# A gated-linear-attention layer with a split-bf16 feed-forward block: gate products moved to GpSimd, matmuls regrouped by PSUM bank, residual input added in the last group

## What is computed

```python
xn = _layernorm(x, axis=-1)
x = x + attn(xn) + relu(xn @ w1 + b1) @ w2 + b2          # w1: 1024x4096, w2: 4096x1024
# attn, 4 heads, dk = 256, dv = 512 per head:
q, k, v = xn @ Wq * dk**-0.5, xn @ Wk, xn @ Wv
gk = log_sigmoid(xn @ Wgk1 @ Wgk2 + bgk2) / 16
S = S * exp(g_t)[:, None] + k_t[:, None] * v_t[None, :];  o_t = q_t @ S    # scan over tokens
o = o * rsqrt(mean(o*o) + eps) * g_norm_weight * silu(xn @ Wg)
attn = o @ Wo
```

## Time and profile before

| | |
|---|---|
| device time, median of 2 runs | 5033.21 us (5014.32 to 5052.1) |
| profiled execution, its own time | 5015.24 us |
| its span on the slowest core (core 2) | 5013.7 us |
| spans of the 8 cores | 4989.3 to 5013.7 us |
| mean granted TensorE clock | 0.850 to 0.859 of full speed |
| TensorE / VectorE / ScalarE / GpSimd busy | 69% / 28% / 16% / 7% |

### The profile page before, as it was taken

One profiled execution on the slowest core, in us unless ns is written; L12 is line 12 of the kernel. 1 busy time (PEld: TensorE's weight loads), 2 busy tenths in 40 slices (PEclk: granted clock), 3 DMA queues, 4 the chain that ended last, 5 costly groups with the idle time before them and its releaser, 6 DMA issues.

```text
span 5013.7 us, 51334 instructions; the slowest of 8 cores (4989.3 to 5013.7 us)
## 1 busy us (share of the span) xinstructions
PE 3447.4 (69%) x17452; PEld 1990.7 (40%) x17640; DVE 1382.9 (28%) x2200; ACT 786.5 (16%) x2034; POOL 370.0 (7%) x758
## 2 busy tenths in 40 slices
PE   2000766866998666866998666866998666866998
PEld 0000435544443435544443435544443435544443
DVE  3343133133222133133222133133222133133222
ACT  4333112111000212111000212111000212111000
POOL 2232100000000000000000000000000000000000
PEclk7555778988999788988999788988999788888999
DMA  6999511211323111210323111111323111101222
GB/s 176 285 291 288 165 35 39 68 34 34 113 93 116 49 41 44 68 34 34 109 96 113 53 41 44 68 34 34 109 94 110 58 40 45 68 26 34 84 93 84
DMA packets 176738, 431.36 MB, mean 86 GB/s; under 512 B 22737, under 2 KB 55633, under 8 KB 176482
## 3 DMA queue, kind: packets, MB, share of 16 engines
q0 software_dynamic: 67584, 234.92, 14.3%
q1 hardware_dynamic: 72034, 159.57, 10.4%
q10 hardware_dynamic: 36864, 33.57, 2.5%
HBM read 352.48 MB, written 75.50 MB: 85 GB/s over the span
## 4 chain that ended last, share of the span: by engine, by line
PE 65%; DVE 13%; DMA 9%; ACT 7%; issue 6%; ACTq 0%; DVEq 0%; POOL 0%; SPq 0%; POOLq 0%
PE pb L900 13%; PE pb L549 7%; PE pb L941 5%; PE pb L944 5%; PE pb L950 4%; DVE k_sils L719 4%; PE pb L792 4%; PE pb L807 3%; PE pb L842 3%; PE pb L848 2%; PE pb L839 2%; PE pb L654 2%; PE pb L787 2%; PE pb L660 2%; PE pb L657 2%
## 5 line engine op out<-in xcount | busy, mean ns | idle before, releaser
L549 PE MATMUL pb<-t_xnfl,w_wqh 128*128 128x512 bf16 x244 | 94.5, 387 | 468.5 <-DMA w_wql<-wq_lo 467.3
L900 PE MATMUL pb<-t_xnfh,w_wvh 128*128 128x512 bf16 x1004 | 382.8, 381 | 44.3 <-DVE t_attn L967 29.4
L941 PE MATMUL pb<-w_wgh,f_h1h 128*128 128x512 bf16 x984 | 372.4, 378 | 51.0 <-DVE k_gg L909 37.9
L944 PE MATMUL pb<-w_wgl,f_h1h 128*128 128x512 bf16 x1024 | 387.7, 379 | 4.6 <-PE pb L950 2.9
L900 PE MATMUL pb<-t_xnfh,w_wvl 128*128 128x512 bf16 x1004 | 383.1, 382 | 1.3
L900 PE MATMUL pb<-t_xnfl,w_wvh 128*128 128x512 bf16 x1000 | 381.7, 382 | 1.5 <-issue 0.4
L787 PE MATMUL pb<-h_v,k_p 128*128 128x256 f32 x256 | 120.5, 620 | 319.2 <-ACT k_otm L696 183.5
L967 DVE SCALAR_TENSOR_TENSOR t_attn<-pb,t_attn 128x512 f32<-128x512 f32 x224 | 146.9, 687 | 587.0 <-PE pb L950 575.0
L654 PE MATMUL pb<-w_wvh,t_xnfh 128*128 128x256 bf16 x1024 | 288.7, 282 | 28.6 <-ACT h_spf L585 28.6
L914 ACT ACTIVATE f_h1h<-k_gg 128x512 bf16<-128x512 f32 x128 | 80.5, 629 | 1408.9 <-DVE k_gg L909 1408.9
L950 PE MATMUL pb<-w_wgh,f_h1l 128*128 128x512 bf16 x1004 | 300.2, 379 | 1.1
(11 more groups left out here) (151 smaller groups left out, 5312.1 us busy)
## 6 DMA issues: line engine op xcount, KB each, us to landing
w_wvh<-w_hi POOLq DMA_DIRECT2D x64, 512.0 KB, 3.7
w_wvl<-w_lo POOLq DMA_DIRECT2D x64, 512.0 KB, 3.6
w_wgh<-w_hi POOLq DMA_DIRECT2D x64, 512.0 KB, 4.1
w_wgl<-w_lo POOLq DMA_DIRECT2D x64, 512.0 KB, 3.6
t_x<-x SPq DMA_DIRECT2D x32, 512.0 KB, 4.7
h_v<-w_l SPq DMA_DIRECT2D x64, 256.0 KB, 12.4
h_g<-w_l SPq DMA_DIRECT2D x64, 256.0 KB, 12.5
w_wvh<-wv_hi POOLq DMA_DIRECT2D x32, 512.0 KB, 3.6
```

The costliest lines, as they stand in the source:

```text
L549: last = t.matmul(pb[bk][:, 0:PW], wgt[:, k * 128:(k + 1) * 128], mov[k][:, sl], start=first, stop=(k == 7 and wgt is wl))
L900: last = t.matmul(pb[bank][:, 0:tile_tok], w_ap, mov[k][:, 0:tile_tok], start=first, stop=(k == 7 and lo_pass))
L941: last = t.matmul(pb[bk][:, 0:512], hh, wgh_cs[jpi][:, wsl], start=(slot == 0), stop=False)
L944: last = t.matmul(pb[bk][:, 0:512], hh, wgl_cs[jpi][:, wsl], start=False, stop=False)
```

## The change

It has three parts. The two gate products L623 and L629 go from VectorE to GpSimd. In the output projection and in the second feed-forward product, the three products of a bank follow each other, where before the two banks' first two products came first and then the low products of both; the same matmuls are issued. The second load of x and its addition go from group 6 to group 7, the last, there for each block between its accumulation and its store.

```diff
@@ emit_gates
-                    OP("vector", lambda v, c2=c2, jt=jt, x=x: v.tensor_tensor(
+                    OP("gpsimd", lambda g, c2=c2, jt=jt, x=x: g.tensor_tensor(
                        out=qt[x][:, c2 * C:(c2 + 1) * C],
...
-                    OP("vector", lambda v, c2=c2, jt=jt, x=x: v.tensor_tensor(
+                    OP("gpsimd", lambda g, c2=c2, jt=jt, x=x: g.tensor_tensor(
                        out=kt[x][:, c2 * C:(c2 + 1) * C],
...
@@ wo_mms
                             last = t.matmul(pb[bk][:, 0:512], oh,
                                             woh_cs[dpart][:, dsl],
-                                            start=(dc == 0), stop=False)
+                                            start=first[dpart], stop=False)
+                            first[dpart] = False
                             last = t.matmul(pb[bk][:, 0:512], oh,
                                             wol_cs[dpart][:, dsl],
                                             start=False, stop=False)
-                        for dpart in range(2):
-                            bk = 2 + dpart
-                            dsl = slice(dc * 512, (dc + 1) * 512)
                             last = t.matmul(pb[bk][:, 0:512], ol,
@@ f2_slot
                             last = t.matmul(pb[bk][:, 0:512], hh,
                                             wgl_cs[jpi][:, wsl],
                                             start=False, stop=False)
-                        for dh in range(2):
-                            bk = 2 * j + dh
-                            wsl = slice(b * 1024 + dh * 512, b * 1024 + dh * 512 + 512)
                             last = t.matmul(pb[bk][:, 0:512], hl,
@@ groups of the feed-forward part
-                if grp == 6:
-                    for j in range(JC):
-                        ob = j % 2
-                        r0 = t0 + j * C
-                        OP("sync", lambda s, ob=ob, r0=r0: s.dma_start(
-                           out=x_c[ob][:], in_=x_hbm[r0:r0 + C, :]),
-                           writes=[f"x{ob}"], dma=True, stream=f"x{ob}")
-                        OP("vector", lambda v, j=j, ob=ob: v.tensor_tensor(
-                           out=attn_c[j][:], in0=attn_c[j][:], in1=x_c[ob][:],
-                           op=ALU.add),
-                           reads=[f"attn{j}", f"x{ob}"], writes=[f"attn{j}"])
             else:
                 for j in range(JC):
+                    ob = j % 2
                     r0 = t0 + j * C
+                    OP("sync", lambda s, ob=ob, r0=r0: s.dma_start(
+                       out=x_c[ob][:], in_=x_hbm[r0:r0 + C, :]),
+                       writes=[f"x{ob}"], dma=True, stream=f"x{ob}")
...
+                    OP("vector", lambda v, j=j, ob=ob: v.tensor_tensor(
+                       out=attn_c[j][:], in0=attn_c[j][:], in1=x_c[ob][:],
+                       op=ALU.add),
+                       reads=[f"attn{j}", f"x{ob}"], writes=[f"attn{j}"])
                     OP("sync", lambda s, j=j, r0=r0: s.dma_start(
                        out=out_hbm[r0:r0 + C, :], in_=attn_c[j][:]),
```

More of the change, by code:

```diff
@@ L832, in wo_mms @@
                     last = None
+                    first = [True, True]
                     for dc in range(4):
```

## The result

| | before | after |
|---|---|---|
| device time, median | 5033.21 us | 5212.59 us (11 runs) |
| ratio to before, 95% interval | | 1.0393 [1.0373, 1.0414] |
| profiled execution, its span | 5013.7 us (core 2) | 5208.8 us (core 0) |
| mean granted TensorE clock of the cores | 0.850 to 0.859 | 0.829 to 0.832 |

The change makes the kernel 3.9% slower. The forecast was 5200 us (5140 to 5290), slower. The ratio of a kernel leaves out disturbed executions, so it can differ from the quotient of two medians.

What follows compares the result with a forecast made beforehand. The prediction saw matmuls bounding the feed-forward part, and chains handed between engines bounding the scan and tile starts. Gate products +126, residual move +65, relief -13 gave +178 us: 5200 us, range 5140 to 5290.

Steps and rivals of the forecast that it cites:

- Part 1: Output projection and second feed-forward product: reordering the matmuls costs 0, with bounds of -10 and +10 us.
- Part 2, block 0: Scan start: block 1's products wait behind weight loads in GpSimd's queue, delaying L764 and L807 by 6.2 us per head.
- Part 2, blocks 2 and 3: Scan, from L608 to L692: GpSimd's dearer products, taken at 0.4 us, add 0.6 us a block, 1.2 us per head.
- Part 2, the clock: Scan: TensorE idles some 8 us more in block 0, so its lower clock adds 0.5 us per head (0 to 1.5).
- Part 3: Last group: x loads queue behind stores, adding 18.4 us at the end and 15.6 at each of three boundaries, +65 us.
- Group 6 gives back: Feed-forward: with the adds gone from group 6, nearly all of L900's 13.8 us of waits for L909 goes, -13 us.
- The sum: Whole kernel: 126 + 65 - 13 = +178 us, about 5200 us.
- B: Gate products on GpSimd cost 1.0 us because they meet VectorE's work: +115 us more, 5315; chance 0.08.
- C: GpSimd works past the waiting loads, so block 0 loses nothing: 5054 us, not tellably slower; chance 0.12.
- D: Last group: x loads mostly hidden, only the adds remain, 20 us instead of 65, 5155 us; chance 0.08.

Runs made afterwards that it cites:

- e_block1_vec: The changed kernel with block 1's four gate products of a head back on VectorE; ratio to the kernel before 1.010.
- e_own_sems: The changed kernel with the hi and lo loads of each weight buffer on semaphores of their own; ratio to the kernel before 1.016.
- e_blocks23_vec: The changed kernel with the gate products of blocks 2 and 3 back on VectorE; ratio to the kernel before 1.0356.
- p2_gates: The kernel before with only the gate products moved to GpSimd; ratio to the kernel before 1.0324.
- p3_again: The kernel before with only the second x load and its addition moved to the last group, timed once more; ratio to the kernel before 1.0065.
- v_order: The kernel before with x additions spread over groups 1 to 4 and the next tile's first two x loads ahead of the stores; ratio to before 0.9904.
- v_split: v_order with hi and lo weight loads on own semaphores and only blocks 0 and 1's gate products on GpSimd; ratio to the kernel before 0.9801.

## Why the prediction was right

**Part 1** cost nothing that shows, as said.

**Part 2, block 0.** Said: 6.2 us a head, since GpSimd's queue holds block 1's products until the last "lo" load is issued and L764 is queued behind L635. Measured: 107.9 / 16 = 6.7, and e_block1_vec and e_own_sems show both links of it. The steps from the first product to L807 take 3.71 us in the mean of the heads instead of the 3.35 said (each pair keeps ScalarE's L635 waiting 0.86 us, where VectorE's kept it 0.45). The rest is that the row of issues ends 10.9 us after the last L680 in the mean, and 10.6 in the head that I read.

**Part 2, blocks 2 and 3.** Said: 0.6 us a block. Measured: 3.53 - 2.71 = 0.82 in the rows of one block, and 0.96 by e_blocks23_vec; the products are dearer than the 0.4 us that I took. The estimate by the Trainium skill ("GPSIMD Engine Reference", section 3.1), 0.47 us a product, was nearer than mine by the nearest rows; the trace agrees with it to 0.02 us.

**Part 2, the clock.** This term was mis-sized: "0.5 us per head (0 to 1.5)". The runs showed 2.0 between blocks 0 and 1 (e_blocks23_vec), outside its range. I had judged it by a mean over a stretch (0.78) and not asked at which level the matmuls right behind the new wait would run. For the products of blocks 2 and 3 and the clock together I had 1.7 us a head; the stage grew by 3.6.

**Part 3.** Said: end +18.4, boundaries +15.6 each. Measured: +16.0 and +14.1 (42.2 / 3), since the stores lie 5.9 to 8.2 us apart over the four tiles, 6.6 in the mean, and not 7.1: a load with one store ahead mostly landed sooner than the 5.3 us that I took.

Group 6 gives back 21 us where I had 13, and this is the clock term a second time. A group of the feed-forward part takes 44.9 us from first accumulation to first accumulation; before, group 7 took 51.4, 50.2, 51.3 and 48.4 in the four tiles, and with the additions moved 44.9 in all. The waits of L900 for L909 are the 13.8 us that I counted. Behind them the granted clock fell to 0.50 for 6.8, 3.4 and 6.8 us in tiles 1 to 3 (not in tile 4). Just behind the wait of the earlier trace rows:

```profile
2713.10:2716.40 3.30, 3.08 (x8) 1.22 (x8) 1.52 (x3) 0.63 (x1) 0.41 (x1) 0.50 0.46 159
```

Half of these 17 us is 8.5, and 13.8 + 8.5 = 22 comes close to the 21 us that came back. So part 3 cost 30 to 37 us, not 52.

**The sum.** That the time came so near is in part luck, since the errors cancel: part 2 came out at some 163 us by p2_gates' ratio (0.0324 x 5013) for the 126 said, part 3 at 33 for 52. The total of 178 stands against 195 by the two profiled spans, 197 by the ratio (0.0393 x 5013) and 179 by the medians.

**The rivals.** B (products at 1.0 us because they meet VectorE's work) fell: the 128 L623 lie between 452 and 468 ns. The rule named for it, of the Trainium skill ("SBUF — State Buffer", "Who interferes with whom"), is not refuted, since VectorE mostly idles while the products run, but it costs nothing here: the gate scan L603 has a median of 415 ns after and 417 before. C fell by the timeline: in none of the 16 heads does a product start between the load issues. D fell by after's rows and by p3_again.

## What to carry to other kernels

A queue that issues DMAs is no free engine: before moving compute onto it, look in its timeline for issues that wait for a landing, and ask what stands behind them and what in turn is queued behind the one who waits for that. Busy shares do not choose what to offload; the instruction that stands between a chain's end and its next link does (here 3.35 us of reciprocal, and not 0.29 us products). When a change adds idle time to TensorE, price the matmuls right behind it at the lower clock; when it takes idle time away, count the clock that comes back too.

## What had not been expected of the hardware

In the head shown of the changed kernel TensorE's granted clock was 0.50 from the first L807 to block 1's L692 (1810.54 to 1821.60), after a wait of 10 us; it was 0.50 behind waits of 3.4 us in the kernel before too (block 0's L787 and L792, and group 7 in three of four tiles). And in one head it fell just behind a wait filled with matmuls up to its last 2.7 us (1.00, then 0.53), while in four heads of the same run it held through both groups. And a two-input product of 128x128 on GpSimd is steady to 4% (452 to 468 ns) over all 128 L623. GpSimd's small products at a tile's start turned out to be held by its weight loads as well, once the x loads came early enough: 13.5 us in v_order against v_split, which nobody had looked for.
